# Swapping the two arms of TensorE's two run-time branches in a one-core GNN and mixer block

## What is computed

```python
xn = _layernorm(x)                                  # x: 1250 nodes x 512, 40000 edges (src, dst)
x = x + gnn(xn, ...) + mixer(xn[None], ...)[0]      # mixer: 2 layers of linear attention and FFN
x = x + ffn(_layernorm(x)[None])[0]

def gnn(x, gate_W, gate_b, Wl, bl, Wr, edge_index): # 4 experts, top 2 of them per node
    ...
    def sage_conv(h, W_l, b_l, W_r):
        aggr = segment_sum(h[src], dst, num_segments=n) * inv_deg
        return aggr @ W_l + b_l + h @ W_r
    for e in range(4):
        h = x
        for l in range(2):
            h = relu(sage_conv(h, Wl[e, l], bl[e, l], Wr[e, l]))
```

## Time and profile before

| | us |
|---|---|
| median of three runs | 1990.46 |
| the three runs | 1989.37, 1990.46, 1996.28 |
| profiled execution, its own time | 1996.28 |
| its span, first to last instruction | 1994.5 |
| granted TensorE clock, mean share | 0.973 |
| TensorE matmul busy | 1817.4 |

### The profile page before, as it was taken

The page is one execution under the profiler, slowest core; times in us unless marked ns, Lnnn a source line. Parts: engine busy times, 40 slices in busy tenths (PEclk is TensorE's granted clock), DMA queues, the critical chain, the costliest instruction groups (busy, mean ns, idle before and its releaser), DMA issues. The chain is left out here.

```text
span 1994.5 us, 26833 instructions
## 1 busy us (share of the span) xinstructions
PE 1817.4 (91%) x9484; PEld 1500.1 (75%) x9484; DVE 865.9 (43%) x1776; ACT 645.4 (32%) x1210; POOL 616.1 (31%) x507
## 2 busy tenths in 40 slices
PE   1798999999999999958999989999989998899993
PEld 1455788888888787847789877887768988778883
DVE  8996311111111146545565446222566554552236
ACT  7844211211111211016536523221364455222210
POOL 4004432423231333015321107433361210154422
PEclk9999999999999999979999999999999999999997
DMA  2168512213121666235702001011175020011102
GB/s 62 43 150 135 66 66 98 76 74 121 53 100 42 223 222 187 87 111 130 226 27 95 22 1 34 31 43 44 38 203 154 27 95 22 1 43 43 56 24 67
DMA packets 112020, 166.45 MB, mean 83 GB/s; under 512 B 42683, under 2 KB 60842, under 8 KB 110898
## 3 DMA queue, kind: packets, MB, share of 16 engines
q1 hardware_dynamic: 111913, 165.05, 28.8%
HBM read 103.24 MB, written 55.53 MB: 80 GB/s over the span
## 5 line engine op out<-in xcount | busy, mean ns | idle before, releaser
L773 PE MATMUL ps<-yT,wslot 128*128 128x500 f32 (+1 forms) x576 | 208.2, 361 | 9.3 <-ACT qpT L1785 6.1
L774 PE MATMUL ps<-yT,wslot 128*128 128x500 f32 (+1 forms) x576 | 206.6, 359 | 0.0
L775 PE MATMUL ps<-yT,wslot 128*128 128x500 f32 (+1 forms) x576 | 206.4, 358 | 0.0
L1016 PE MATMUL ps<-g,adj 125*128 125x512 f32 (+1 forms) x800 | 186.4, 395 | 1.7 <-DVEq L1151 1.2
L2136 POOL TENSOR_TENSOR wslot<-mix_landing,wslot 128x512 fp32r<-128x512 f32 x96 | 126.7, 1350 | 186.8 <-ACT wslot L1722 186.8
L1016 PEld LDWEIGHTS ps<-g,adj 125*128 125x128 f32 (+1 forms) x800 | 150.1, 188 | 38.1 <-DVEq L1151 1.6
L2141 POOL TENSOR_TENSOR hidT<-qpT,hidT 128x500 fp32r<-128x500 f32 (+1 forms) x96 | 102.9, 1075 | 214.1 <-DVE hidT L1926 214.1
L1785 ACT ACTIVATE qpT<-ps,all_cols 128x500 f32<-128x500 f32 (+1 forms) x96 | 58.0, 609 | 313.9 <-PE ps L775 266.8
L773 PE MATMUL ps<-parts,w 128*128 128x500 f32 (+1 forms) x384 | 135.4, 353 | 2.3 <-PEq L558 2.3
L774 PE MATMUL ps<-parts,w 128*128 128x500 f32 (+1 forms) x384 | 135.4, 353 | 0.0
L775 PE MATMUL ps<-parts,w 128*128 128x500 f32 (+1 forms) x384 | 135.4, 353 | 0.0
(11 more groups left out here) (291 smaller groups left out, 3689.4 us busy)
## 6 DMA issues: line engine op xcount, KB each, us to landing
mix_landing<-in_L_mix_W SPq DMA_DIRECT2D x16, 1024.0 KB, 5.1
qk_dram<-qk_parts SPq DMA_DIRECT2D x128, 125.0 KB, 2.4
g_dram<-staged SPq DMA_DIRECT2D x40, 256.0 KB, 2.0
u_dram<-staged SPq DMA_DIRECT2D x40, 256.0 KB, 2.0
g_in<-g_dram SPq DMA_DIRECT2D x40, 256.0 KB, 3.6
u_in<-u_dram SPq DMA_DIRECT2D x40, 256.0 KB, 2.7
k_stack<-qk_dram SPq DMA_DIRECT2D x8, 1250.0 KB
q_stack<-qk_dram SPq DMA_DIRECT2D x8, 1250.0 KB
```

Of the source, the lines that this page charges most:

```text
L773: nc.tensor.matmul(out, lhs_high, rhs_high, start=first, stop=False)
L774: nc.tensor.matmul(out, lhs_high, rhs_low, start=False, stop=False)
L775: return nc.tensor.matmul(out, lhs_low, rhs_high, start=False, stop=last)
L1016: last = nc.tensor.matmul(m.ps[0:counts.shape[1], t % 2, :], counts if exact else counts.bitcast(F32), part if exact else part.bitcast(F32 ...
```

## The change

Both conditions are turned round and their arms swapped. The same arm runs as before; in the instruction stream it stands second now, and the arm that never runs with these inputs stands first.

```diff
                 top_sum = pe.value_load(m.top_sum[0:1, 0:1], min_val=0, max_val=E)
-                with pe.If(top_sum <= EXACT_COUNTS):
+                with pe.If(top_sum > EXACT_COUNTS):
+                    sums(False)
+                with pe.Else():
                     sums(True)
-                with pe.Else():
-                    sums(False)
...
                 top_sum = pe.value_load(m.top_sum[0:1, 0:1], min_val=0, max_val=E)
-                with pe.If(top_sum <= EXACT_COUNTS):
+                with pe.If(top_sum > EXACT_COUNTS):
+                    all_counts_times_g(False)
+                with pe.Else():
                     all_counts_times_g(True)
-                with pe.Else():
-                    all_counts_times_g(False)
```

## The result

The changed kernel takes 2003.23 us in the median of 13 runs (1997.29 to 2012.81), the kernel before 1990.46 us in 13 runs (1987.24 to 1998.36). The ratio is 1.006 with a 95% interval of 1.0046 to 1.0074: slower by 0.6% (12.8 us between the medians), where 4.4 us had been forecast and 2001 us was the upper end of the range. The profiled execution took 2002.15 us with a span of 2000.3 us.

A forecast was written before the change was run, and what follows sets the result against it. TensorE was taken to bound the kernel, its matmuls busy 1817.4 of 1994.5 us. The terms 0 + 0 + 4.2 + 0 + 0.2 = 4.4 us on 1990.46 gave 1994.9 us, range 1990 to 2001.

The forecast's parts named there:

- Both exits: Ends of the two branches, before lines 773 and 1574: removing the far jump gains 0 at each.
- the second entry: Line 1029: jump hidden under queued matmuls, barely; 0.2 us, with 0 and 0.8 as bounds.
- DMA adjT<-kept: Before line 602: the DMA named by the page as ending the 2.06 us wait; the prediction saw TensorE's sequencer chain instead.
- Entry of the first branch: the full jump is exposed: Line 631, before line 602: no queued matmul covers the jump, so 4.2 us go through to the barrier.
- 3.61 us and 0.6 for the DMA load: First entry: larger exit jump less 0.087 us, plus 0.6 us for DMA load, making 4.2 us.
- the upper bound of 9 us: First entry: whole time from the branch to 185, if the fetch waits for all transfers ahead; some 9 us.
- 0 with bounds of -2 and +1.5: First stage after the entry: clock effect of TensorE's later start taken as 0 us, between -2 and +1.5.
- the clock stays at half: Rival at the first entry: long half-clock stretch loses up to 13 us, total 17.4 us, 2007.9 us; chance 0.04.
- a half stretch beyond 190: Sign of being wrong: the clock's half stretch after the first entry lasts beyond 190 us.
- it had been nearly idle before: Clock step at the first entry: TensorE's half clock until about 182 us was put beside its earlier near idleness.
- 1.4 to 11.3 us: Whole kernel: the forecast's own bounds on the added time, the upper end with little chance.
- The chance of 0.06 for slower by over 0.5%: Whole kernel: 0.04 from the clock and 0.02 from the upper ends; the same had 0.93.

The follow-up runs named there:

- e2_second_only: Only the second branch's swap applied to the kernel before; 1990.65 us, ratio 0.999.
- e11_no_branch: Kernel before with both branches, both register loads and both fp32 arms left out; 1987.52 us, ratio 0.9977.
- e4_dma_held: Changed kernel with weight loads and stores of counts held back until the degrees are summed; 1992.49 us, ratio 1.0013 to the kernel before.
- e5_pad40: Changed kernel with 80 waits that never run (40 instructions) at the end of the first branch's dead arm; 1995.76 us, ratio 1.0022 to the kernel before.
- e12_pad10: Changed kernel with 20 waits that never run (10 instructions) at the end of the first branch's dead arm; 2003.6 us, ratio 1.0054 to the kernel before.
- e1_first_only: Only the first branch's swap applied to the kernel before; 2001.02 us, ratio 1.0051.
- e3_near_target: Changed kernel with the first branch's dead arm cut to a single wait, so the jump lands near by; 1987.22 us, ratio 0.998 to the kernel before.
- e7_before_busy: Kernel before with 10 idle matmuls at the end of the count stage and 8 in front of the first branch; 1987.47 us, ratio 0.9978.

## Why the prediction was wrong

**Three of the four places were right.** Both exits gained nothing and the second entry was hidden: the waits before lines 773, 1574 and 1016 stayed at 2.2, 3.5 and 1.2 us, and `e2_second_only` shows the second entry in the median as well. The page's "DMA adjT<-kept" before line 602 was rightly not followed (`e11_no_branch`). That the first entry would be exposed was right too; its price was not.

**The step that failed is "Entry of the first branch: the full jump is exposed".** Its term of 4.2 us was mis-sized: from the branch to line 773 the changed kernel lost 76.5 - 66.0 = 10.5 us. Two things were wrong in it, the price of the jump under load and the belief that a far jump is one wait, and the clock hangs on the second.

*The jump itself.* I took 3.61 us and 0.6 for the DMA load; it was 6.187 - 0.087 = 6.1 us. The load was worth 2.3 us (`e4_dma_held`: 3.9 us at a share of 0.02 against 6.2 at 0.90), nearly four times what I gave it. It had been seen in the earlier trace rows and sized by feeling; the upper bound of 9 us held it. In the traces a near jump of 0.25 us goes without a packet on q8, and the far jumps of 3.9 us without and 6.2 us with load have one each. By the Trainium skill, page Runtime: NRT & Kernel Launch, section Instruction fetch mechanics, a taken branch to a target outside the two pages that are held waits for a DMA fetch. For the far jumps the traces agree. The loop of 528 matmuls jumps back in 0.2 us because what it needs is at hand all the same: in the kernel before q8 has no packet from 330 to 692 us, so that three of its four turns ran on instructions that had been fetched once.

*The second stop.* 2.8 us were in no step. I had costed a far jump as one wait. `e5_pad40` and `e12_pad10` show that it is a jump and then, if the landing is shortly before a certain place of the stream, a second stop, whose length falls by what TensorE still has to do until then: 9 matmuls left 2.8 us, 4 matmuls 4.4 us. The second packet on q8 shows what is waited for, and `e4_dma_held` that it took the DMA load for it to be late. A hint stood in the trace of the kernel before: at each of its two hidden far jumps q8 has two packets, 3.3 and 3.5 us apart. Whether the place of the stop is exactly the end of the first packet's instructions no view shows.

*The clock.* I set 0 with bounds of -2 and +1.5. It was 1.8 us on line 602. `e5_pad40` has the same jump without the second stop and its matmuls take 8.15 us, 0.6 less than before; so for the jump alone the 0 was about right, and the second stop brought the rest. The stop costs 5.2 us in all by this pair (76.5 against 71.3): 2.8 standing and 2.4 in slower matmuls. The rival "the clock stays at half" had the sign right, but not the size: 1.2 GHz until 194 us, for some 10 us of which TensorE was standing anyway (175 to 182 and 186 to 189). The prediction's own sign of being wrong, a half stretch beyond 190, came true. Its "it had been nearly idle before" holds for 170 to 175 us alone; at 165 to 170 TensorE was busy for 4.67 of 5 us.

**The range.** 6.1 + 2.8 + 1.8 = 10.7 us is explained. The medians differ by 12.8, with an interval of 9.2 to 14.7 us by the ratio, and by 9.2 us in `e1_first_only`. The upper end of 2001 allowed for 10.5. I had called the forecast's bounds 1.4 to 11.3 us and then given the upper part "little chance", though the one row that bore on it, a DMA share of 0.79 to 1.02 against 0.03, pointed there. The chance of 0.06 for slower by over 0.5% was far too small.

**What stays open.** Why `e3_near_target` is 4.6 us below the kernel before in the median (interval 0.8 to 7.2) with line 773 at the same time; why the medians of `e4_dma_held` and `e5_pad40` are 1.4 and 2.2 us less above their kernel before than line 773 says, and that of `e7_before_busy` 1.8 us further below. The clock later in the kernel may be all of it: the mean granted clock is 0.979 in the median of the runs of `e3_near_target` and 0.977 in those of its kernel before. Why it should differ, no run tells. What holds the first packet back under load, and why TensorE goes on only 1.6 to 1.9 us after a packet has landed, stays open too.

## What to carry to other kernels

Put the arm that will run first, so that the far jump comes at its end, where the sequencer is ahead of the matmuls or a barrier waits anyway; an entry behind a register load has nothing queued to hide it. When a jump has to be exposed, look at the DMA load at that moment, and in the changed kernel's trace for a second stop shortly behind the landing, with a packet of the instruction queue in it; a few instructions that never run can move the landing past that place (here 40, worth 5.2 us by line 773). A stand can cost the clock as well. A few idle matmuls over the two short stands of TensorE at 170 to 176 us were cheap and made the kernel before 0.2% faster; under the far jump they gained nothing that can be told.

## What the runs showed of the hardware that I had not expected

- A far jump of TensorE's sequencer took 3.3 to 3.9 us where the DMA share was between 0.02 and 0.22, and 6.1 to 6.5 us at a DMA share near 0.9; a jump over a few instructions took 0.25 us.
- A far jump shows as one packet of 16384 bytes on queue q8 within the branch, and a second one that starts 3 to 7 us after the first. In the changed kernel and in `e12_pad10` the second stop ended 1.9 us after that second packet had landed.
- A loop with 528 matmuls in its body jumped back in 0.2 us, and q8 had no packet from 330 to 692 us.
- Ten more instructions that never run moved a stop of TensorE from behind its ninth to behind its fourth matmul, and forty removed it.
- An fp32 matmul of 128 columns stands in the trace as two matmuls (10 written, x20 recorded).
- The stand of 2.1 us at the first branch of the kernel before, behind one of 2.8 us at the start of the stage, cost 2.6 us more in slower matmuls: with TensorE kept busy over both, or without the branch and so with the first stand alone, line 602's 30 matmuls took 6.14 and 6.17 us in place of 8.77.
